# Two edits to the start and the middle of a masked multi-head attention: early shifted scores for the first head, and row maxima over half the columns for every other tile of the later heads

## What is computed

```python
logits = einsum('bhqd,bhkd->bhqk', q, k) / sqrt(DK)     # layer 2: + log(clip(adj, 1e-8)); layer 3: + (2*adj - 1)
attn   = softmax(logits, axis=-1)                       # layer 3: weights * (0.25 + 0.75*adj), renormalised
out    = einsum('bhqk,bhkd->bhqd', attn, v)             # then Wo, bias, residual, layer norm (layer 3: a feed-forward too)
```

## Time and profile before

| what | value |
|---|---|
| median of 3 runs | 4511.79 us (4506.36 to 4515.14) |
| profiled execution | 4507.2 us, span in the trace 4505.4 us |
| PE busy, share of the span | 4099.7 us, 91% |
| DVE busy | 3033.0 us, 67% |
| ACT busy | 2211.1 us, 49% |
| POOL busy | 1924.4 us, 43% |
| mean granted TensorE clock | 0.955 of full speed |
| chain that ended last | PE 56%, issue 17%, POOL 14%, DVE 7%, ACT 3% |

### The profile page before, as it was taken

One profiled execution on the slowest core, in us unless ns is written; L12 is line 12 of the kernel. 1 busy time (PEld: TensorE's weight loads), 2 busy tenths in 40 slices (PEclk: granted clock), 3 DMA queues, 4 the chain that ended last, 5 costly groups with the idle time before them and its releaser, 6 DMA issues.

```text
span 4505.4 us, 69471 instructions
## 1 busy us (share of the span) xinstructions
PE 4099.7 (91%) x21040; PEld 2192.1 (49%) x21040; DVE 3033.0 (67%) x5152; ACT 2211.1 (49%) x3894; POOL 1924.4 (43%) x1064
## 2 busy tenths in 40 slices
PE   7998999989999899998999989998999989999898
PEld 6534365344753447543474434744347443564334
DVE  3687737877378764787647876478755787557774
ACT  3365533655336553465534655246543465435663
POOL 1174701746027560265503655036540465404563
PEclk9998999999999999999999999999999999999999
DMA  3201102011020110201102011120111101111010
GB/s 106 75 18 32 52 17 70 18 34 50 25 62 17 34 50 30 59 15 36 48 30 59 15 36 49 33 57 13 38 50 34 52 13 39 52 36 50 10 41 15
DMA packets 106289, 176.57 MB, mean 39 GB/s; under 512 B 27296, under 2 KB 50336, under 8 KB 105888
## 3 DMA queue, kind: packets, MB, share of 16 engines
q1 hardware_dynamic: 105888, 171.69, 13.3%
HBM read 83.12 MB, written 8.39 MB: 20 GB/s over the span
## 4 chain that ended last, share of the span: by engine, by line
PE 56%; issue 17%; POOL 14%; DVE 7%; ACT 3%; SPq 2%; DMA 1%; POOLq 0%; DVEq 0%; ACTq 0%
POOL region_p L1446 11%; PE ps L706 9%; PE ps L573 9%; PE ps L565 9%; PE ps L625 8%; PE ps L675 7%; PE ps L654 6%; PE ps L792 4%; PE ps L614 2%; DVE region_p L1181 2%; POOL rstd L1456 1%; SPq L475 1%; DMA region_k<-region_p 1%; POOL y_t L1515 1%; SPq L399 1%
## 5 line engine op out<-in xcount | busy, mean ns | idle before, releaser
L1446 POOL TENSOR_TENSOR region_p<-region_p,mask 128x1024 f32<-128x1024 f32 x608 | 1444.8, 2390 | 489.9 <-ACT region_p L920 488.9
L1195 DVE TENSOR_REDUCE row_max_bf<-ps 128x1 bf16<-128x1024 f32 x768 | 939.7, 1224 | 197.2 <-PE ps L675 184.9
L706 PE MATMUL ps<-region_p,shelf 128*64 128x512 f32 x3584 | 949.7, 600 | 5.1 <-ACT o_raw L943 5.1
L920 ACT ACTIVATE region_p<-ps 128x512 f32<-128x512 f32 x1216 | 664.2, 596 | 349.0 <-PE ps L654 346.8
L654 PE MATMUL ps<-region_q,region_k 97*64 97x512 bf16 x4096 | 715.3, 401 | 24.2 <-DVE region_p L1181 15.3
L675 PE MATMUL ps<-region_k,region_q 96*64 96x512 bf16 x3584 | 593.7, 399 | 7.8 <-DVE row_max_bf L1191 7.8
L1181 DVE TENSOR_TENSOR region_p<-ps,mask 128x512 f32<-128x512 f32 x832 | 529.7, 680 | 76.4 <-ACT ps L916 76.1
L916 ACT ACTIVATE ps<-ps 128x512 f32<-128x512 f32 x832 | 445.9, 580 | 260.4 <-PE ps L654 254.4
L1456 POOL TENSOR_TENSOR rstd<-var_eps,minus_half 128x2 f32<-128x2 f32 (+1 forms) x160 | 116.9, 730 | 972.2 <-DVE var_eps L1127 972.2
L654 PEld LDWEIGHTS ps<-region_q,region_k 97*64 97x64 bf16 x4096 | 255.0, 112 | 463.7 <-DVE region_p L1181 195.5
L675 PEld LDWEIGHTS ps<-region_k,region_q 96*64 96x64 bf16 x3584 | 200.8, 113 | 428.4 <-issue 385.7
(11 more groups left out here) (160 smaller groups left out, 5342.0 us busy)
## 6 DMA issues: line engine op xcount, KB each, us to landing
mask<-in_adj SPq DMA_DIRECT2D x64, 512.0 KB, 7.4
mask<-in_adj_t SPq DMA_DIRECT2D x64, 512.0 KB, 3.4
y_t<-o_raw SPq DMA_DIRECT2D x224, 64.0 KB, 2.0
sums_t<-o_raw SPq DMA_DIRECT2D x224, 64.0 KB, 2.0
region_q<-region_p SPq DMA_DIRECT2D x192, 64.0 KB, 2.0
region_k<-region_p SPq DMA_DIRECT2D x192, 64.0 KB, 2.0
region_q<-sums_t SPq DMA_DIRECT2D x192, 64.0 KB, 2.0
region_k<-sums_t SPq DMA_DIRECT2D x192, 64.0 KB, 2.0
```

Source lines behind the costliest of these rows:

```text
L706: last = nc.tensor.matmul(ps[64 * c:64 * c + 64, VALUE_BANK, :], values_and_one, probs[:, t % RING, c * HALF:(c + 1) * HALF], start=(t == ...
L920: nc.scalar.activation(probs[:, t % RING, c * HALF:(c + 1) * HALF], scores_t, ACT.Exp, scale=DK ** -0.5).then_inc(exp_done, 1)
L1195: nc.vector.tensor_reduce(row_max_bf[i][:, t:t + 1], flat[:, (t % 2) * N:(t % 2 + 1) * N], AX.X, ALU.max)\
L1446: nc.gpsimd.tensor_tensor(p, p, mask[:, t, :], ALU.mult).then_inc(masked_pool, 1)
```

## The change

1. `HEAD_START = 2`: the shifted scores of head 0's tiles 0 and 1 (4 matmuls each) and their exponentials (2 each) are issued right behind the last two maxima of head 1: PE's order becomes maximum (1,6), scores (0,0), maximum (1,7), scores (0,1), and then for head 2 the maxima (2,0) and (2,1) with no scores behind them. ACT takes the exponentials of (0,0) between the Relus of (1,6) and (1,7). The waits for the loads of heads 2 and 3 and for the row of -1 move ahead of scores (0,0). DVE's and POOL's orders stay, so DVE masks (0,1) behind the maximum of (2,1) as before.
2. `LEAD_TILES`: tiles 1, 3, 5 and 7 of heads 2 to 7 take their maximum over 512 columns too. POOL makes four key differences ahead of the first mask (two before), and one more behind the mask of tile 3 of heads 0 to 3; PE waits for the difference before such a tile.
3. POOL's loop over pairs of heads is written out.

```diff
-LEAD_TILES = {0: tuple(range(T)), 1: tuple(range(T))}
+LEAD_TILES = {h: tuple(range(T)) if h < 2 else (1, 3, 5, 7) for h in range(H)}
+HEAD_START = 2
@@ PE
+            def shifted_scores(b, layer, h, t):
+                if t == 0:
+                    pe.wait_ge(max_row_in[h % 2], max_rows_in(b, layer, (0, h + 2), h % 2))
+                for c in range(2):
+                    wait_bank(b, layer, ("scores", h, t, c))
...
             def head(b, layer, h):
...
                     if h < H - 2:
                         scores_for_maximum(b, layer, (0, h + 2), t)
-                    if t == 0:
...
+                    if h or t >= HEAD_START:
+                        shifted_scores(b, layer, h, t)
@@ PE, heads(): behind each maximum of head 1
-                pe.wait_ge(ones_loaded, b * 16 + 16)
-                for h in range(2, 4):
-                    head_loaded(b, layer, h)
+                    if t >= T - HEAD_START:
+                        if t == T - HEAD_START:
+                            pe.wait_ge(ones_loaded, b * 16 + 16)
+                            for h in range(2, 4):
+                                head_loaded(b, layer, h)
+                        shifted_scores(b, layer, 0, t - (T - HEAD_START))
@@ ACT, behind each take_lead of head 1
+                        if t >= T - HEAD_START:
+                            exponentials(b, layer, 0, t - (T - HEAD_START))
@@ ACT, head(): 
+                    if h or t >= HEAD_START:
+                        exponentials(b, layer, h, t)
@@ POOL
+            def key_difference(b, layer, h):
+                pool.wait_ge(aug_loaded[h], b * AUG_COUNT + 16 * AUG_DMAS * (layer + 1))
+                pool.sem_inc(passed, 1)
+                nc.gpsimd.tensor_tensor(k_diff[0:AUG - 1, h, :], k_aug[0:AUG - 1, h, 0:HALF],
+                                        k_aug[0:AUG - 1, h, HALF:N], ALU.subtract).then_inc(k_diff_ready, 1)
...
+                    if t == 3 and h < H - 4:
+                        key_difference(b, layer, h + 4)
...
-                    for h in LEAD_TILES:
...
+                    for h in range(4):
+                        key_difference(b, layer, h)
```

More of the change, by code:

```diff
@@ L640, in wait_bank @@
                     pe.wait_ge(exp_done, att(b, layer, (0, before[1]), 2 * T, 2 * before[2] + before[3] + 1))
+            def shifted_scores(b, layer, h, t):
[3 more added lines that the diff above has]
+                    wait_bank(b, layer, ("scores", h, t, c))
+                    for m in range(2):
+                        last = nc.tensor.matmul(ps[64 * m:64 * m + 64, BANKS["scores", h, t, c], :],
+                                                k_aug[0:AUG, h, t * P + 64 * m:t * P + 64 * m + 64],
+                                                q_aug[0:AUG, h, c * HALF:(c + 1) * HALF],
+                                                start=True, stop=True)
+                    last.then_inc(st_done, 1)
             def head(b, layer, h):
@@ L903, in adjacency_exp, with exponentials @@
                                      scale=2.0).then_inc(e_ready, 1)
+            def exponentials(b, layer, h, t):
+                for c in range(2):
+                    act.wait_ge(st_done, att(b, layer, (0, h), 2 * T, 2 * t + c + 1))
+                    scores_t = ps[:, BANKS["scores", h, t, c], :]
+                    if t in DVE_TILES[h]:
+                        nc.scalar.activation(scores_t, scores_t, ACT.Exp, scale=DK ** -0.5).then_inc(exp_done, 1)
+                    else:
+                        if c == 0:
+                            act.wait_ge(pv_done, att(b, layer, (0, h), T, t - RING + 1))
+                        nc.scalar.activation(probs[:, t % RING, c * HALF:(c + 1) * HALF], scores_t, ACT.Exp,
+                                             scale=DK ** -0.5).then_inc(exp_done, 1)
             def head(b, layer, h, exps=()):
@@ L1492, in whole @@
                         pool.wait_ge(g3_ready, b * T + T)
-                    for h in LEAD_TILES:
-                        pool.wait_ge(aug_loaded[h], b * AUG_COUNT + 16 * AUG_DMAS * (layer + 1))
-                        pool.sem_inc(passed, 1)
-                        nc.gpsimd.tensor_tensor(k_diff[0:AUG - 1, h, :], k_aug[0:AUG - 1, h, 0:HALF],
-                                                k_aug[0:AUG - 1, h, HALF:N], ALU.subtract).then_inc(k_diff_ready, 1)
+                    for h in range(4):
+                        key_difference(b, layer, h)
                     wait_all_emptied(pool, b, ("v2", "v3")[layer], 4)
@@ L1503, in whole @@
                         pool.wait_ge(g_ready, b * T + T)
-                    for h in range(2):
-                        head(b, layer, (0, h))
-                    with pool.Fori(1, H // 2 - 1) as pair:
-                        for i in range(2):
-                            head(b, layer, (pair, i))
-                    for h in range(H - 2, H):
-                        head(b, layer, (0, h))
+                    for h in range(H):
+                        head(b, layer, h)
                     for half in range(2):
```

4 lines of the change are left out of this document (2 added, 2 removed).

## The result

The changed kernel takes 4521.43 us (median of 16 runs, 4516.83 to 4535.56) where the kernel before, in 16 runs beside it, takes 4510.41 (4506.36 to 4518.37). The ratio is 1.0025, 95% interval 1.0018 to 1.0032: slower, by a quarter of a percent.

What follows compares the result with a forecast made beforehand. PE was taken to bound heads 1 to 5, and the chain between PE, ACT and DVE to count at layer starts. 5.6 us (tile 1) plus 4.0 (starts) made 9.6 more than 4511.79, forecast 4520, range 4490 to 4546.

Steps and rivals of the forecast that it cites:

- PE bounds the middle heads, DVE's work doesn't: Heads 1 to 5: PE, busy 73.69 of 75.20 us, sets the end; DVE, busy 64.81, is close behind.
- The hop over ACT, 0.07 at 80 tiles: Tile 1, heads 1 to 5, 16 layers: the mask starts 0.07 us later through ACT's Relu, 5.6 us slower in all.
- pairs at tile 2 0.65 apart: Sign in a middle head: PE's two pairs of score matmuls at tile 2 start about 0.65 us apart.
- DVE's work is not on the path, so what counts is when the masks of tiles 1, 4 and 6 start.: Middle heads: 207 us less DVE work gains nothing by itself; only these masks' start times matter to PE.
- the 75.2 to 75.8 that I named as a sign: Sign: heads 1 to 5 together take 75.2 to 75.8 us; under 74.5 would prove the prediction wrong.
- Tiles 4 and 6, POOL's key differences: nothing: Middle heads: waits behind masks of tiles 4 and 6 stay, and POOL's 96 added differences are covered; no time either way.
- The start, 0.25 a layer: Layer starts: early scores delay scores (0,2) through ACT's queue, 0.25 us a layer, 4.0 us slower over 16 layers.
- Maximum (1,6) on PE as before ... Scores (0,0) from 2079.68: First step at layer 1's start: maximum at 2079.22 as before, its Relu at 2079.67, then the early scores at 2079.68.
- the pause behind (2,0): Sign at a layer's start: PE stands still for about a microsecond after the maximum (2,0).
- the clock comes back later: Layer starts: later values miss the clock's return, 1.5 us more a layer, 4544 or 4532 us; chance 0.22.
- the clock stays full: Layer starts: eight more matmuls keep the clock full until the values start, 30 us faster, 4488 with part 1; chance 0.16.
- DVE is let go: Middle heads: shorter maxima free DVE's masks, tile 2's wait shrinks 0.29 us, 4489 us, or -58 with all 0.72 gone; chance 0.10.

Runs made afterwards that it cites:

- e12: Kernel before with only DVE's order changed (tile 1: mask halves before the maximum; tiles 4, 6: maximum between them); 4514.93 us, single run.
- e7: Changed kernel without early scores, DVE's masks and maxima reordered at tiles 1, 4, 6, later shorter maxima only at 4, 6 and head 7's tile 7; 4484.56 us.
- e11: Changed kernel with tile 1's maximum over 1024 columns again in heads 2 to 7; 4518.1 us, single run.
- e3: Changed kernel without early scores and, of all later maxima, only head 7's tile 7 over 512 columns; 4515.59 us, ratio 1.0009.
- e1: Changed kernel without the early scores, so the shorter maxima alone; 4509.80 us, ratio 0.9999.
- e2: Changed kernel with all later maxima over 1024 columns again, so the early scores alone; 4530.79 us, ratio 1.0048.
- e5: Kernel before with four extra unread matmuls behind each of head 1's last six maxima; 4501.07 us, ratio 0.9974.
- e4: Changed kernel with the early scores moved behind maximum (1,7) and their exponentials behind its Relu; 4536.23 us, ratio 1.0047.
- e6: Changed kernel with four extra unread matmuls behind each of head 1's last six maxima and behind maxima (2,0) and (2,1); 4498.99 us, ratio 0.9970.
- e9: e4 with the extra unread matmuls of e6; 4478.81 us, ratio 0.9930.
- e10: e7 with the extra unread matmuls of e5, and four more at each of head 0's tiles 0, 1 and 2; 4423.32 us, ratio 0.9808.

## Why the prediction came out

The time was right, 4520 said and 4521 measured, and so was the sign of the likeliest sum. But that was in part luck: of its terms one was nearly right, one was three times too small and one was missing.

- **PE bounds the middle heads, DVE's work doesn't.** Right. 190 us less of it moved the four heads by +2.7. That PE's waits there are mostly a matter of the place of DVE's masks, and less of how much DVE does, was not in the prediction; e12 (28.7 us by the order alone) and e7 (40.1 with two shorter maxima in the new order) show it.
- **The hop over ACT, 0.07 at 80 tiles.** The mechanism is shown by e11 and the size was a little large: 0.042, so 80 x 0.042 = 3.4 instead of 5.6 us. The Relu starts 0.42 after the scores, not the 0.45 that I took from a start, where PE's pair behind an idle time takes 0.41 instead of 0.38 us (the earlier trace rows and 1926.83). The sign that I named, pairs at tile 2 0.65 apart, was wrong: both pairs wait for the mask, so both move, and they stay 0.59 apart.
- **"DVE's work is not on the path, so what counts is when the masks of tiles 1, 4 and 6 start."** A step that failed. A fourth place waits for DVE, head 6's tile 0 behind head 7's last maximum, and the change cut 0.53 us a layer there: -8.4 us (e3, e11). The row stood in the trace of before with a bracket naming DVE, and its sum of 8.9 us in the line group of L654; I had read one middle head and not the last one. This is also why the five heads took 74.90 us, less than the 75.2 to 75.8 that I named as a sign.
- **Tiles 4 and 6, POOL's key differences: nothing.** Right: e11, which keeps the maxima of tiles 3 and 5 and the differences, has 962.94 against 962.83 in four heads.
- **The start, 0.25 a layer.** Its size was 0.76 in the mean (12.2 / 16), and two steps failed. The first is "Maximum (1,6) on PE as before ... Scores (0,0) from 2079.68": I had granted full clock until 2082.0 because that is where it fell before. In layer 1 of the fourth graph it fell earlier, before (0,0), and matmuls at half clock in front of the exponentials added 0.62 of the 0.81 (0.94 worked out, 1.56 measured); the chain itself (exponentials before Relu (1,7), maximum (2,1), mask (0,1), scores (0,2)) is in the trace, step by step. That start has as much half clock as before, 6.8 us in both kernels, but now half of it lies in the chain. So two signs failed as well: the pause behind (2,0) did not come, and scores (0,2) started more than half a microsecond later. The second step is the sum itself, 0.25 x 16 with no start late: six more were. What moved the clock is open.
- **Rival "the clock comes back later".** It happened, in part of the starts, and makes some 8 of the 12.2 us. In layer 0 six starts of eight are late (13.7 us at half clock), where before one at each end was and the six between had 10.2; in layer 1 two are (28.18 and 27.61 us, where before both took 25.90). The price, 1.35, is near the 1.5 of the prediction. My estimate of what decides it, half a microsecond of delay, is not borne out: in layer 1 of the fourth graph the values start 0.8 later after the turning and the clock is back in time. Over all starts half clock went from 149 to 153 us only; what counts is where it lies. How much of this is the edit's doing is not shown: with the starts untouched 2, 4 and 6 are late (before, e1, e3), with the early scores 8, 12 and 14 (after, e11, e2), in one profiled execution each.
- **Rival "the clock stays full".** It did not happen by itself. With extra products in the gaps it does, and then it pays: 0.9974 in the order of before.
- **Rival "DVE is let go".** Not by less work. Let go by the order of DVE's masks, PE gains 40.1 us in four heads (e7), 0.63 a head, between the rival's 0.29 and 0.72.
- **The sum.** From the first turning of a layer to the last: 12.2 + 2.7 - 7.8 = 7.1 us, against 9.6 predicted, and 11.0 between the medians. What is left, 4 us, I do not attribute: stages that e3 and e5 do not touch moved by more, and the starts that e3 leaves alone moved by 8.1. An undersized loss and an overlooked gain nearly cancelled, and the total alone would have confirmed a wrong account.

**Where the starts' loss comes from otherwise.** The early scores have little to gain: mask (0,1) waits for the maxima (2,0) and (2,1) wherever scores (0,0) stand, and e4, e6 and e9 show that setting anything ahead of those delays it, through ACT or through PE. How much of it would be left at full clock without extra products was not measured.

The Trainium skill ("TensorE: Matmul & The Clock Gate", "A second HAM failure mode: psum-queue depth-cycling") says that short idle times between groups of matmuls, as PSUM banks go round, can make the clock change to and fro. The starts agree: they have gaps of 0.75 us and the clock is at half for 149 us in them, and with the gaps filled it stays full (0 us in e9 and e10). The Trainium skill ("PSUM — Partial Sum Buffer", "Engine vs sequencer instructions") calls the queues of ScalarE, VectorE and GpSimd strictly first in, first out; the Relu behind two exponentials here (2090.03) and the 28.7 us of e12's order agree.

## What to carry to other kernels

When an engine's work shrinks, list every place where another engine waits for it, the first and last rounds of a loop too, and ask at each whether the wait is for the amount or for the place in its order; here the order alone was worth 28.7 us in four heads, the shorter maxima 8 at one place, and 11 more only once the order was changed. A chain through a stretch with a changing clock must be worked out at both levels, since an edit can move the stretch onto the chain. And where the matrix engine idles for fractions of a microsecond beside a chain of other engines, try filling the gaps.

## What was not expected of the hardware

- Matmuls that nobody reads made the program faster: 576 more of them, a better order and a few shorter maxima took 2% off (e10; without the extra products it is 0.6%, e7), and with the order of before six groups a layer took 0.26% off (e5).
- The half-clock time in the starts changes with edits elsewhere: e3, which leaves the starts alone, had 177 us of it where before and e1 had 149; e7 and e12, which leave the last maxima of head 1 alone and give head 0's masks another order, had 203 and 206. So a gain in one stage can be lost again in another, as in e12, where 28.7 us gained in the heads, 27.5 lost in the starts and 7.2 at head 6 left nothing.
- A start at full clock throughout is 24.2 us in the order of before; with 6.8 us at half it was 25.9, with 10.2 26.7, with 13.7 27.7 and 28.2. Where the half clock falls counts too: in e1, 6.8 us of it went with starts of 25.41 and of 27.56. Through all kernels without extra products the time of the starts goes with the number of late ones, from 2 (425.6 us) to 16 (453.1, e12).
- One program's executions differ by it too: those of e4 run from 4513.83 us at a mean granted clock of 0.956 to 4546.77 at 0.944.
